# Moving keys, values, a row scatter and two shared products into the routing programs of a two-layer kernel

## The reference

```python
x = x + tanh(g_xattn[0]) * L0_xattn(layernorm(x), ctx, ctx, ...)   # 16 heads, causal, 1601 keys
x = x + tanh(g_ffn[0]) * L0_ffn(layernorm(x), ...)                 # 8 experts of width 1024, top 2
x = x + tanh(g_xattn[1]) * L1_xattn(layernorm(x), ctx, ctx, ..., mask)
x = x + tanh(g_ffn[1]) * L1_ffn(layernorm(x), ...)                 # 16 experts of width 352, top 2,
                                                                  # capped capacity, + shared MLP
```

## Time and profile before

| | us |
|---|---|
| median of 3 runs | 1684.55 |
| lowest, highest | 1681.94, 1687.09 |
| profiled execution | 1685.84 |
| its span in the trace | 1684.1 |

### The profile page before, as it was taken

One profiled execution on the slowest core, in us unless ns is written; L12 is line 12 of the kernel. 1 busy time (PEld: TensorE's weight loads), 2 busy tenths in 40 slices (PEclk: granted clock), 3 DMA queues, 4 the chain that ended last, 5 costly groups with the idle time before them and its releaser, 6 DMA issues. The chain is left out here.

```text
span 1684.1 us, 25789 instructions
## 1 busy us (share of the span) xinstructions
PE 1479.1 (88%) x8703; PEld 905.5 (54%) x8704; DVE 857.4 (51%) x2028; ACT 679.1 (40%) x1109; POOL 415.2 (25%) x348
## 2 busy tenths in 40 slices
PE   4678999999999756999999999559999766999996
PEld 2433333333232645999999999312333454666664
DVE  3579998878870643222232323668887364211110
ACT  3213556667677221333323333215778321122221
POOL 0020000089930053111111111020000306136554
PEclk9869999999999867999999999758999876999998
DMA  3730505026306443136913131240100401245553
GB/s 116 251 80 20 158 20 150 18 102 202 130 21 186 165 154 106 26 100 159 229 25 102 25 103 22 85 132 21 33 27 2 138 8 51 68 109 144 141 136 47
DMA packets 107474, 160.39 MB, mean 95 GB/s; under 512 B 16008, under 2 KB 89724, under 8 KB 105215
## 3 DMA queue, kind: packets, MB, share of 16 engines
q1 hardware_dynamic: 72063, 100.99, 19.9%
q0 software_dynamic: 22528, 48.87, 11.8%
q10 hardware_dynamic: 12800, 9.48, 2.0%
HBM read 101.76 MB, written 58.20 MB: 95 GB/s over the span
## 5 line engine op out<-in xcount | busy, mean ns | idle before, releaser
L793 DVE TENSOR_REDUCE mxp<-psA 128x1 f32<-128x384 f32 (+4 forms) x640 | 334.9, 578 | 66.1 <-PE psA L649 45.8
L767 ACT ACTIVATE Pt<-psC 128x1024 f32<-128x1024 f32 (+4 forms) x296 | 256.2, 918 | 156.3 <-PE psC L675 80.8
L649 PE MATMUL psA<-Kst,Qst 97*128 97x384 bf16 (+4 forms) x640 | 182.7, 352 | 34.3 <-DVE mxp L793 18.4
L1673 PE MATMUL psA<-xTt,OT 128*128 128x128 f32 x1728 | 202.2, 277 | 4.4 <-issue 4.1
L1673 PEld LDWEIGHTS psA<-xTt,OT 128*128 128x128 f32 x1728 | 197.3, 193 | 11.2 <-issue 11.2
L793 DVE TENSOR_REDUCE mxpt<-psA 128x1 f32<-128x449 f32 x256 | 145.2, 619 | 35.4 <-PE psA L649 30.4
L649 PEld LDWEIGHTS psA<-Kst,Qst 97*128 97x128 bf16 x640 | 55.6, 100 | 179.9 <-DVE mxp L793 131.0
L675 PE MATMUL psC<-Qst,Kst 100*128 100x512 bf16 (+4 forms) x592 | 151.2, 360 | 0.7 <-ACT Pt L767 0.2
L1623 POOL DMA_INDIRECT residual<-yv,lab x36 | 56.0, 1555 | 355.3 <-DVE yv L1782 289.5
L1770 DVE SCALAR_TENSOR_TENSOR hT<-psA,b,sil 128x128 f32<-128x128 f32 x216 | 64.1, 345 | 155.2 <-ACT sil L1743 155.2
L767 ACT ACTIVATE Ptt<-psC 128x1024 f32<-128x1024 f32 (+1 forms) x128 | 123.8, 1020 | 47.5 <-PE psC L675 47.1
(11 more groups left out here) (316 smaller groups left out, 2016.9 us busy)
## 6 DMA issues: line engine op xcount, KB each, us to landing
rows<-blank SPq DMA_DIRECT2D x4, 4386.0 KB, 17.3
OT<-L_w SPq DMA_DIRECT2D x8, 2048.0 KB
mi<-mask POOLq DMA_DIRECT2D x16, 800.5 KB
Kst<-k_parts SPq DMA_DIRECT2D x12, 800.5 KB, 15.6
w<-L_w SPq DMA_DIRECT2D x8, 1024.0 KB
Qst<-q_parts SPq DMA_DIRECT2D x48, 128.0 KB, 2.8
Qstt<-q_parts SPq DMA_DIRECT2D x48, 128.0 KB, 2.8
wg<-L_w_gate POOLq DMA_DIRECT2D x16, 352.0 KB
```

Source lines behind the costliest of these rows:

```text
L649: mmi = pe.matmul(out, Qst[0:KA, half[u] % QN, at:at + P], Kst[0:KA, h, k0:k0 + w], start=True, stop=diag is None and not masked)
L767: act.activation(Pt[0:kw, n % SLOTS, :, col:QC], psC[0:kw, n % 2, :].rearrange("p (y t) -> p y t", y=2)[:, :, col:QC], ACT.Exp).then_inc(p ...
L793: dve.tensor_reduce(mxp[:, q, h, pc:pc + 1], psA[:, place_of[("piece", n)] % AB, 0:w], AX.X, ALU.max).then_inc(a_free, 1)
L1673: mmi = pe.matmul(bank(j)[:, i * P:(i + 1) * P], w1[:, side, k, f * P:(f + 1) * P], xTt[:, z, k, :], start=(k == 0), stop=(k == KD - 1))
```

## The change

- First projections: ScalarE waits for the variance and takes the root as its first work; the bias scaling and the key copies stand behind it.
- Logits by expert: the router matrix becomes the stationary operand and 512 rows stream past it, 2 products for each of four row groups, into banks 0 and 1. ScalarE copies the [experts, 512] result to `lgT`, and TensorE transposes it back to rows in bank 6, from which `choose` reads as before.
- First routing: keys and values of layer 1 run inside this program, three key pieces ahead of the second `positions` and five behind it, then the values (banks 2 and 3); VectorE's value additions and splits stand behind `tables`; SyncE stores the parts; GpSimd runs the second scatter and waits until all scatters have landed. The first experts' program starts without all this.
- Second routing: TensorE computes the first two shared products at its end; `experts1` goes on with the third.

```diff
@@ first projections, scalar
                         if ql is not None:
+                            act.wait_ge(lnv, 1)
+                            act.activation(lnw[:, 3, :], lnw[:, 2, :], ACT.Sqrt).then_inc(lns, 1)
                             act.wait_ge(ldq, 32)
                             act.activation(bq[:, :], bq[:, :], ACT.Copy, scale=0.25).then_inc(bq4, 1)
-                            act.wait_ge(bq4, 1)
...
                             if kind == "q" and m == 0:
-                                act.wait_ge(lnv, 1)
-                                act.activation(lnw[:, 3, :], lnw[:, 2, :], ACT.Sqrt).then_inc(lns, 1)
+                                act.wait_ge(bq4, 1)
@@ project_and_route, sync
                         places["loads"](sp, ot, NC * NG, up)
+                        if L == 0:
+                            places["keys"]["store"](sp)
@@ project_and_route, gpsimd
                         scatter(pool, 0)
                         pool.wait_ge(slots_s, 2)
+                        if L == 0:
+                            scatter(pool, 1)
+                            scattered(pool)
@@ project_and_route, scalar
+                        def logits_out(c):
+                            act.wait_ge(lgm, c + 1)
+                            if c >= 2:
+                                act.wait_ge(lgt, 1)
+                            act.activation(lgT[:, c % 2, :], bank(c % 2)[0:E, :], ACT.Copy).then_inc(lge, 1)
...
                         turned("x", 1)
+                        logits_out(0)
+                        logits_out(1)
                         turned("a", 3)
...
                         turned("x", 3)
+                        logits_out(2)
+                        logits_out(3)
+                        if L == 0:
+                            places["keys"]["pieces_out"](act, range(0, 1))
                         exponentials(1)
+                        if L == 0:
+                            act.wait_ge(mm, 2 * NC)
+                            places["keys"]["pieces_out"](act, range(1, 8))
@@ project_and_route, tensor
-                        def logits(h):
+                        def logits(c):
...
+                            for k in range(KD):
+                                mmi = pe.matmul(bank(c % 2)[0:E, :], wr[:, k, :], places["xT"][:, k, c * QC:(c + 1) * QC],
+                                                start=(k == 0), stop=(k == KD - 1))
+                            mmi.then_inc(lgm, 1)
+
+                        def logits_back(h):
+                            for c in (2 * h, 2 * h + 1):
+                                pe.wait_ge(lge, c + 1)
+                                for q in range(QTC):
+                                    t = c * QTC + q
+                                    mmi = pe.transpose(bank(6)[:, t * E:(t + 1) * E], lgT[:, c % 2, q * P:(q + 1) * P],
+                                                       ident[0:E, 0:E])
                             mmi.then_inc(lgt, 1)
...
+                        logits(2)
+                        logits(3)
+                        logits_back(1)
+                        if L == 0:
+                            pe.wait_ge(up, 2 * NC)
+                            places["keys"]["pieces"](pe, range(0, 3))
                         positions(1)
+                        if L == 0:
+                            places["keys"]["pieces"](pe, range(3, 8))
+                            places["keys"]["values"](pe)
+                        else:
+                            places["shared"](pe)
@@ project_and_route, vector
                             places["tables"](dve, link, bank(7)[:, 2 * E * HT:2 * E * HT + E], cst)
+                            places["keys"]["split"](dve)
@@ second_keys, vector: the values first, then the splits
+                for j, (k0, kw) in enumerate(key_tiles()):
+                    dve.wait_ge(vmm, j + 1)
+                    dve.tensor_tensor(Vaug[0:kw, j, :, 0:DH], bank(2 + j % 2)[0:kw, 0:D].rearrange("p (h d) -> p h d", h=H),
+                                      bvb[0:kw, :].rearrange("p (h d) -> p h d", h=H), ALU.add).then_inc(vev, 1)
                 for m in range(NJ):
@@ experts0
                         mask_gpsimd(pool)
-                        scatter(pool, 1)
...
-                        keys_sync(sp)
...
-                        keys_tensor(pe)
...
-                        keys_scalar(act)
-                        scattered(act)
...
-                        keys_vector(dve)
@@ layer 1
+                def shared_begin(pe):
+                    pe.wait_ge(w_ld[SHARED], 64)
+                    for m in range(2):
+                        shared_up(pe, 0, m)
```

117 lines of the change are left out of this document (57 added, 60 removed).

## The result

The changed kernel takes 1664.03 us (median of 4 runs, 1662.69 to 1669.59) against 1684.17 before (4 runs, 1681.94 to 1687.09): a ratio of 0.988, 95% interval 0.986 to 0.990, about 20 us. The profiled execution took 1663.77 us with a span of 1661.8. The forecast was 1671.0 with a range from 1664 to 1680: the sign was right, the time lies at the low edge of the range, and the gain is 6 to 7 us larger than the sum.

A forecast was written before the change was run, and what follows sets the result against it. Matrix engine busy 88% of the span, but the gain was sought at three seams where engines wait for one another. Terms -10.5 - 4 + 0.5 = -14.0 from the median 1684.55 give 1670.6, said as 1671; range 1664 to 1680.

The forecast's parts named there:

- Part A: First projections: taking the root first starts attention at about 73 instead of 83.7, about -10.5 us.
- store-bound: Rival, first projections: the last query store keeps its 16 us, so 7.3 us gained there, about 1675 in all; chance 0.2.
- Part B: First routing and the keys, values and scatters it absorbs: about -4 us, experts begin near 650.
- At the second seam GpSimd decides: First routing to experts' program: GpSimd's scatters, with 5.01 us idle between the halves, set when the expert loop begins.
- Neither reaches the sum: GpSimd is still at its first half: First routing, logits by expert: first half's 0.5 us and second half's 3 us earlier or 2 later gain nothing.
- The contention term: First routing: VectorE's key splits beside GpSimd's second 16 scatters slow them by 5.5 us, kept whole.
- Part C: Second routing: GpSimd sets the program's end and the moved shared products are worth nothing; about +0.5 us.
- unmoved seams: Rival: attention waits for an unmoved transfer or the long routing costs 4 us more to leave; about 1682; chance 0.06.
- slower: Rival, first routing: value additions and tables also block descriptor writing, scatters take 51 us; 1687 to 1690; chance 0.04.
- Free scatters: Rival, first routing: scatters run freely beside the splits, -7.5 us there, end about 1668; chance 0.12.

The follow-up runs named there:

- e2: Kernel before with logits by expert alone, nothing moved across a seam: 1678.0 us, ratio 0.996.
- e5: Kernel before with root first and logits by expert, nothing moved across a seam: 1667.4 us, ratio 0.988.
- e12: Changed kernel unchanged, timed again with a second profile: 1665.0 us, ratio 0.987.
- e3: Changed kernel with the first two shared products back at the head of the last program: 1668.0 us, ratio 0.989.
- e6: Changed kernel with VectorE's 16 residual additions in the last program taken in fours behind every third hidden tile: 1662.6 us, ratio 0.986.
- e9: Changed kernel with VectorE's 16 residual additions taken two by two behind each of hidden tiles 1 to 8: 1659.9 us, ratio 0.985.
- e10: Changed kernel with the six key splits and the key stores moved back behind the seam into the experts' program: 1663.1 us, ratio 0.987.
- e11: Changed kernel with residual additions two by two, and key splits and stores back in the experts' program: 1656.4 us, ratio 0.983.
- e4: Changed kernel with the first routing's second-half scatter and its landing wait back in the experts' program: 1686.7 us, ratio 1.001.
- e7: Changed kernel with VectorE's key splits, and the value additions with them, waiting until the whole scatter has landed: 1687.3 us, ratio 1.001.
- e8: Kernel before, unchanged, once more with a profile: 1685.8 us in its one run.
- e1: Kernel before with ScalarE's root first in the first projections, nothing else: 1674.5 us, ratio 0.995.

## Why the prediction was nearly right

**Part A** (forecast -10.5, bounds -11 to -7.3): measured -11.4, from 92.1 on the mean of three profiles to 80.7 of eleven. The steps up to VectorE's last tile went as said, each a little sooner: the query products start at 37.00 rather than 38, the last split ends near 58 rather than 59.4, the last value tile at 71.05 rather than 72.1. But the end was read from the wrong transfer. The forecast has the transfers over at 69 and VectorE last; in all eleven profiles with the edit the last query store lands last, at 71.1 to 72.9, and the next program begins 0.5 us behind it. It takes 13.3 to 13.9 us, between the two cases that the forecast kept, so the rival "store-bound" was wrong in its 16 us and right in what it named. In before it was the other way round: that store landed at 82.36, and SyncE then waited for the last key load, to 83.11.

**Part B** (forecast -4): from R1 to the loop the three profiles of before take 120.2 us on the mean, the five with the moves and the new logits 116.0. The size is right, the account behind it is not. The step that failed is "At the second seam GpSimd decides", and with it "Neither reaches the sum: GpSimd is still at its first half". VectorE's `tables` decided, 0.49 us before the new program, and they hang on the second choice; GpSimd's 5.01 us were a wait for them and not the price of a crossing. So the second half did reach the sum in the kernels with the seam in its old place: e2 and e5 get there without a move. I priced the moves against 5.01 us; beside the new logits GpSimd idles 2.50 and 3.41, and the way from the end of the last DMA to the row load, which I had put at up to 4 us, took 5.5 to 5.8 in after, e12, e3, e6, e9, e10 and e11, and 2.4 to 2.6 in the kernels with the seam in its old place. That eats the gain. Besides, the first scatter comes 9.2 us behind the first choice, 10.6 to 11.8 before: 1.4 us and more, not 0.5; the projection that VectorE's residual waits for ran at 2.4 GHz.

The contention term was right in kind and in size: 5.5 us forecast, 4.1 or 5.6 by the profile, measured against e4 and e7. The Trainium skill (SBUF — State Buffer, "Who interferes with whom") does not agree with this trace where it infers that `tensor_tensor` took only the read interface and left descriptor writing alone: the DMA at 622.64 lies beside a `TENSOR_TENSOR` of 1.83 us and nothing else of VectorE, and takes 2.29 us. (That DMA reads its row places, `slot`, from SBUF, so the section's sentence on reads may cover it; no run here tells the two apart.) Following the row and not the rule was right. The sentence on reads, that two inputs in SBUF contend with a GpSimd instruction that reads SBUF, agrees with the label copy (1.45 us). The value additions, with one input in PSUM, disturb nothing, as it says.

**Part C** (forecast +0.5): from the first choice to loop 2 it is 108.9 to 109.1 us in after, e12 and e4, and 108.9 to 109.0 in before, e8 and e1: 0. The new logits bring the last program 1.1 us forward (41.7 to 40.6) and loop 2 then comes 0.7 later behind it; the moved products put 0.4 back, since they end the program and not GpSimd. The reason given, 16 additions ahead of the hidden tile, is shown by e6 and e9.

**What was missing** is the stretch of the second routing ahead of the first choice. The forecast gave it nothing, and it is 3.4 us shorter on the mean (46.3 to 42.9). The sum of the means is -11.4 - 4.2 - 3.4 + 0 = -19.0, the medians give -20.1.

So the rivals: "unmoved seams" and "slower" did not happen, and "store-bound" only as said above. "Free scatters" did not either, though its time, 1668, was nearer: the scatters were slow beside the splits. A total near a rival's says nothing for the rival.

## What to carry to other kernels

Before pricing a move across a seam, look which engine ended last ahead of it, since the idle time of another engine is not the seam's price, and ask what else in the same change shortens the wait it removes: two remedies for one wait are not added, and here the smaller one, matmuls of 512 columns for matmuls of 16 or fewer, was enough. Moved work counts only as far as its consumer can take it: look at what the engine that reads it does first in the new program. Where executions of one kernel differ by more than the effect, cut the trace into stretches between common instructions and compare those over all profiles.

## What the runs showed of the hardware

- The granted clock of one piece of code differs between executions of the same kernel: projection groups of 16 records at 3.72 or at 5.4 to 6.3 us. The two profiled executions of the changed kernel (1663.8 and 1673.0 us, mean granted clock 0.940 and 0.932) differ by 9.2 us, of which 3.4 lie in the first routing up to the loop and 3.8 in the second up to its first choice.
- How far a new program stands behind the last work of the one before differed with whose work that was: 0.5 us behind the landing of the last store (first projections, eleven profiles), 0.49 to 0.54 behind VectorE's last instruction (first routing of before, e8, e1, e5), 0.31 behind TensorE's last record (second routing with the moved products), 3.28 and 3.29 behind GpSimd's last indirect DMA (second routing of e3, e2 and e5), and 4.67 to 5.00 behind that DMA where GpSimd also waits for its landing (first routing of after, e12, e3, e6, e9, e10 and e11).
- VectorE instructions with two inputs in SBUF held GpSimd's indirect DMA up to their end: 2.29 us for 0.98 beside the split at 622.25, and 4.82 us at 1391.72 (3.25 in e12, where it was issued later) beside the 16 residual additions, which end at 1395.67; all three DMAs are over about 0.9 us after VectorE. Not every DMA beside them was held: the one at 1390.20 took 1.22 us, and in e12 the first two took 1.22 and 1.26. With e9's pairs of additions none takes over 1.23 us.
- TensorE after an idle of 3.02 us still ran at 2.4 GHz (e6), after 7.51 us it restarted at 1.2 GHz (after).
